# State-space stage of a decoder layer: the residual added by TensorE as transposes of x in the output unit's accumulation, and copied out by ScalarE

## What is computed

```python
hs = x @ W_in_states.T;  gate = x @ W_in_gates.T           # 1024 channels
hs = silu(causal_conv(hs, 4 taps) + conv_b)
dt = softplus((hs @ W_dt.T) @ W_dtproj.T + b_dtproj);  B = hs @ W_b.T;  C = hs @ W_c.T
s[l] = exp(A * dt[l]) * s[l-1] + dt[l] * B[l] * hs[l]      # 16 states for each channel
y = sum over the states of s * C + hs * D
out = (y * silu(gate)) @ W_out.T
x1 = x + out                                               # then the layer norm
```

## Time and profile before

| | |
|---|---|
| median of 3 runs | 3223.22 us (3222.08 to 3226.16) |
| the profiled execution | 3223.97 us, span 3222.1 us |
| state-space stage | 0 to 1747 us of the span |
| busy share of the span | PE 93%, DVE 87%, ACT 75%, POOL 65% |

### The profile page before, as it was taken

The page is one execution under the profiler, slowest core; times in us unless marked ns, Lnnn a source line. Parts: engine busy times, 40 slices in busy tenths (PEclk is TensorE's granted clock), DMA queues, the critical chain, the costliest instruction groups (busy, mean ns, idle before and its releaser), DMA issues. The chain is left out here.

```text
span 3222.1 us, 47346 instructions
## 1 busy us (share of the span) xinstructions
PE 3000.6 (93%) x16101; PEld 1827.8 (57%) x16134; DVE 2795.2 (87%) x3637; ACT 2410.8 (75%) x4531; POOL 2094.2 (65%) x1207
## 2 busy tenths in 40 slices
PE   7899999999999999999985899999999999699998
PEld 5777677777777677777753344444444443244444
DVE  6999999999999999999996878777887877288886
ACT  4888888888888888888872377677677667577786
POOL 5999999999999999999995243343344333100000
PEclk9999999999999999999996899999999999899999
DMA  4102220222012210222024455555556553221111
GB/s 173 45 32 79 80 73 18 79 83 79 26 65 79 80 62 29 79 80 83 15 96 137 148 171 168 186 158 177 177 154 179 168 178 92 82 93 47 46 42 36
DMA packets 164385, 311.93 MB, mean 97 GB/s; under 512 B 22736, under 2 KB 80208, under 8 KB 164000
## 3 DMA queue, kind: packets, MB, share of 16 engines
q1 hardware_dynamic: 158784, 299.53, 29.0%
q10 hardware_dynamic: 5360, 9.38, 1.0%
HBM read 217.16 MB, written 91.69 MB: 96 GB/s over the span
## 5 line engine op out<-in xcount | busy, mean ns | idle before, releaser
L830 POOL TENSOR_TENSOR bu<-du,bc 128x1024 f32<-128x1024 f32 x512 | 1198.9, 2370 | 30.4 <-DMA bc<-bc_scratch 28.5
L708 ACT ACTIVATE states<-dt,negA 128x256 f32<-128x256 f32 x2048 | 853.1, 463 | 238.7 <-DVE hc L926 227.9
L914 DVE TENSOR_TENSOR_SCAN states<-states,bu 128x512 f32<-128x512 f32 x704 | 821.5, 1213 | 10.6 <-ACT states L708 8.7
L1565 DVE TENSOR_REDUCE mmax<-s_ps 128x2 f32<-128x1024 f32 x512 | 624.8, 1224 | 205.6 <-PE s_ps L1284 186.7
L1409 ACT ACTIVATE pt<-s_ps 128x512 f32<-128x512 f32 x1024 | 573.5, 598 | 293.6 <-PE s_ps L1293 280.4
L926 DVE TENSOR_TENSOR hc<-states,bc 128x512 f32<-128x512 f32 x704 | 446.4, 676 | 0.4 <-DMA bc<-bc_scratch 0.4
L526 PEld LDWEIGHTS y_ps<-id_sb,hc 128*128 128x128 f32 x2816 | 331.5, 143 | 121.7 <-DVE hc L926 56.1
L526 PE MATMUL y_ps<-id_sb,hc 128*128 128x128 f32 x2816 | 377.5, 277 | 22.1 <-DVE hc L926 22.1
L1293 PE MATMUL s_ps<-qst,kst 105*128 105x512 bf16 x1024 | 379.1, 384 | 15.5 <-ACT pt L1409 5.1
L839 POOL TENSOR_TENSOR hp<-hp,bc 128x1024 f32<-128x1024 f32 x160 | 379.5, 2372 | 1.8 <-DVE hp L914 1.8
L914 DVE TENSOR_TENSOR_SCAN hp<-states,bu 128x512 f32<-128x512 f32 x320 | 372.5, 1206 | 5.2 <-ACT states L708 5.2
(11 more groups left out here) (172 smaller groups left out, 4237.4 us busy)
## 6 DMA issues: line engine op xcount, KB each, us to landing
bc<-bc_scratch SPq DMA_DIRECT2D x128, 512.0 KB, 5.1
stack_d<-parts SPq DMA_DIRECT2D x180, 256.0 KB, 3.0
qst<-stack_d SPq DMA_DIRECT2D x64, 384.0 KB
kst<-stack_d SPq DMA_DIRECT2D x64, 384.0 KB
x<-xres SPq DMA_DIRECT2D x31, 512.0 KB, 5.3
w_raw<-in_w_ffn SPq DMA_DIRECT2D x48, 256.0 KB, 2.7
w_raw<-in_w_ffn SPq DMA_DIRECT2D x16, 768.0 KB, 7.3
xT_sb<-in_xT SPq DMA_DIRECT2D x16, 512.0 KB, 6.0
```

The costliest lines, as they stand in the source:

```text
L708: a = act.activation(states[:, bank, first:first + SEQ], dt[:, t, :], ACT.Exp, scale=negA[:, t, c * NS + n:c * NS + n + 1])
L830: pool.tensor_tensor(bu[:, buf, :].rearrange("p (n l) -> p n l", n=NS), du[:, t % (2 * GRP):t % (2 * GRP) + 1, :].to_broadcast([P, NS, SEQ ...
L914: dve.tensor_tensor_scan(dst, src, bu[:, BU_OF[k][0], cols], 0.0, ALU.mult, ALU.add).then_inc(scan_done, 1)
L1565: dve.tensor_reduce(mmax[:, u // HG, c:c + 2], s1_ps[:, pair], AX.X, ALU.max).then_inc(s1_free, 1)
```

## The change

x is no longer loaded in rows of tokens for the sum, but once more from `xT`, where channels are rows: `xres` becomes [128, 2, 4, 128], and its load is two DMAs of 256 KB with runs of 512 bytes in place of one of 512 KB with runs of 2 KB. At the end of each `o` unit PE adds four transposes of 128x128 of `xres` to the same accumulation (with the identity as the other operand), after a wait for the load. ACT copies the bank to `xres` in `evacuate`, at the place that the table gives (after the decays of step 27 and of step 0). The last batch's `o` is still copied by DVE, now without an addition. The array `x` is no longer an input.

```diff
@@ load_xres (SP)
-                sp.dma_start(xres[:, :, :], at(x, b).rearrange("(i p h) -> p i h", p=P, h=HID)).then_inc(xres_in, 16)
+                src = at(xT, b).rearrange("(p k i l) -> i p k l", p=P, k=HK, i=SEQT)
+                for i in range(SEQT):
+                    sp.dma_start(xres[:, i], src[i]).then_inc(xres_in, 16)
@@ unit (PE)
                     elif kind == "o":
-                        m = pe.matmul(proj[:, :], y[:, par, k, i * P:(i + 1) * P], wout_sb[:, k, :], start=start, stop=stop)
+                        pe.matmul(proj[:, :], y[:, par, k, i * P:(i + 1) * P], wout_sb[:, k, :], start=start, stop=False,
+                                  skip_group_check=True)
+                if kind == "o" and hi == n:
+                    pe.wait_ge(xres_in, (f + 1) * SEQT * 16)
+                    for k in range(HK):
+                        m = pe.matmul(proj[:, k * P:(k + 1) * P], xres[:, i, k, :], id_sb[:, :], start=False, stop=(k == HK - 1),
+                                      is_transpose=True, skip_group_check=True)
@@ evacuate and its caller (ACT)
+                elif kind == "o":
+                    act.activation(xres[:, i].rearrange("p k l -> p (k l)"), proj[:, :], ACT.Copy).then_inc(ev["o"], 1)
-                        if kind != "o":
-                            evacuate(bank, kind, i, batch, side)
+                        evacuate(bank, kind, i, batch, side)
@@ body and tail (DVE)
-            def add_residual(bank, b, i):
-                dve.wait_ge(mm["o"], seq("o", b, i))
-                if i == 0:
-                    dve.wait_ge(xres_in, (b + 1) * 16)
-                dve.tensor_tensor(xres[:, i, :], xres[:, i, :], proj_banks[:, bank, :], ALU.add).then_inc(ev["o"], 1)
+            def last_out(i):
+                dve.wait_ge(mm["o"], seq("o", BATCH - 1, i))
+                dve.tensor_copy(xres[:, i].rearrange("p k l -> p (k l)"), proj_banks[:, 1 + i, :]).then_inc(ev["o"], 1)
-                    for bank, kind, i, batch, _ in due(b, par, k):
-                        if kind == "o":
-                            add_residual(bank, batch, i)
```

More of the change, by code:

```diff
@@ L140, with state_space_phase @@
     assert GRP * CPT * (_j - 1) - 1 <= _at < GRP * CPT * _j, (_j, _at)
-def state_space_phase(nc, xT, x, w_in, w_bc, w_dt, w_dtproj, w_out, chan, ident, w_ffn, bc_scratch, w_scales, x1,
+def state_space_phase(nc, xT, w_in, w_bc, w_dt, w_dtproj, w_out, chan, ident, w_ffn, bc_scratch, w_scales, x1,
                       ctxt, mask, wq, wk, chan_qk, stack_d, mask_d, x1n_d):
@@ L174, in state_space_phase @@
         xT_sb = sb("xT_sb", [P, HK, SEQ])
-        xres = sb("xres", [P, SEQT, HID])
+        xres = sb("xres", [P, SEQT, HK, P])
         xpad = sb("xpad", [P, 2, TAPS - 1 + SEQ])
@@ L357, in load_xres @@
             def load_xres(b):
-                sp.dma_start(xres[:, :, :], at(x, b).rearrange("(i p h) -> p i h", p=P, h=HID)).then_inc(xres_in, 16)
+                src = at(xT, b).rearrange("(p k i l) -> i p k l", p=P, k=HK, i=SEQT)
+                for i in range(SEQT):
+                    sp.dma_start(xres[:, i], src[i]).then_inc(xres_in, 16)
             def store_x1(b):
-                sp.dma_start(at(x1, b).rearrange("(i p h) -> p i h", p=P, h=HID), xres[:, :, :]).then_inc(x1_out, 16)
+                sp.dma_start(at(x1, b).rearrange("(i p h) -> p i h", p=P, h=HID),
+                             xres.ap().rearrange("p i k l -> p i (k l)")).then_inc(x1_out, 16)
             def load_piece(b, i):
@@ L453, in _ @@
                 sp.wait_ge(ev["o"], seq("o", BATCH - 1, i))
-                sp.dma_start(last[:, i], xres[:, i]).then_inc(x1_out, 16)
+                sp.dma_start(last[:, i], xres[:, i].rearrange("p k l -> p (k l)")).then_inc(x1_out, 16)
             sp.wait_ge(x1_out, BATCH * 16 + 16)
@@ L983, in tail @@
                 for i in range(SEQT):
-                    add_residual(1 + i, BATCH - 1, i)
+                    last_out(i)
             over_batches(dve, front, body, tail)
@@ L1994, in build @@
     x1n_d = dram("x1n_d", (BATCH * SEQ * HID,))
-    state_space_phase(nc, ins["xT"], ins["x"], ins["w_in"], ins["w_bc"], ins["w_dt"], ins["w_dtproj"], ins["w_out"],
+    state_space_phase(nc, ins["xT"], ins["w_in"], ins["w_bc"], ins["w_dt"], ins["w_dtproj"], ins["w_out"],
                       ins["chan"], ins["ident"], ins["w_ffn"], dram("bc_scratch", (2 * STATES, SEQ)), w_scales, x1,
@@ L2021 @@
     arrays = {
-        "x": x,
         "xT": x.reshape(BATCH, SEQ, HK, P).transpose(0, 3, 2, 1).reshape(BATCH, SEQ, HID),
```

## The result

| | before | changed |
|---|---|---|
| median, 5 runs each on one chip | 3223.71 us | 3253.93 us (3248.76 to 3257.79) |
| ratio, 95% interval | | 1.0093 (1.0079 to 1.0107) |
| the profiled execution | 3223.97 us | 3257.79 us, span 3256.0 us |

The changed kernel is slower by 30 us; the forecast was 21. The profiled execution of the changed kernel is the slowest of its five. Of its 33.9 us more of span, 31.2 lie in the state-space stage: the fill that follows the stage's tail on DVE starts at 1748.09 us before and at 1779.27 after. The other 2.7 us lie behind the stage, and a second profile of the same kernel, shown further down, doesn't have them, so nothing ties them to the change.

The account below looks back on a forecast made before the run. It took POOL's 104.22 us a batch as the bound, with PE's cycle growing to 104.7. The longer cycle, boundary and tail add 6 us and clock falls 15: 21 on the profiled 3223.97, median 3244, range 3223 to 3256.

Parts of the forecast that it names:

- What bounds the kernel: State-space stage: POOL's own work, 104.22 us a batch, sets the period, so less DVE work can't shorten it.
- The cycle of 104.02: Second cycle before the change, in us: DVE from step 4 to o1's addition, PE's d1, ACT to `xpad`, PE's c0 to step 4's sum.
- rival D: Faster: with DVE resting more, 42 large POOL operations shorten by 20 ns each, gaining 8 us, to 3215; chance 0.05.
- The transposes, 0.87 us a batch: On PE, eight pipelined transposes a batch add 0.87 us, 0.43 for each output unit, none hidden.
- The wait that goes and the one that comes: Batch boundary: d1 stops waiting for DVE; c0 waits for `xpad` behind o1's copy, a 9.5 us path, starting 0.9 us later.
- The period without the clock: State-space stage: PE's new cycle takes 104.7 us a batch, 0.5 over POOL's 104.22, before any clock falls.
- rival B: The cycle is longer but the clock holds: 6 us slower, 3229 (3226 to 3232); chance 0.21.
- The clock: PE idles 2.7 us ahead of c0; nine falls to 1.2 GHz in thirteen batches, 1.7 us each, cost 15 us.
- The rule against the forecast: The skill warns only of longer PE idle gaps; by it the clock holds, but rows at 2.03 and 2.18 us speak against it.
- The boundary and the tail: Last batch: DVE two additions ahead, -1.2 us; POOL's wait shorter, -0.6; tail's transposes, +0.9.
- DMA, nothing: Load of x: one more DMA and shorter runs cost nothing; were it three times slower, 6 us once.
- Rival E: Worse: ACT's wait for o0 delays step 28's scan, or transposes behind a 512-column matmul aren't pipelined; over 3256, chance 0.06.

Follow-up runs that it names:

- LAG 2: Against the changed kernel, ACT copies the output units one step later, o1 behind the decays of step 1: 3224.01 us, ratio 1.0000 to the kernel before.
- the kernel with the stretch filled: The changed kernel plus five matmuls of 256 columns, read by nothing, ahead of c0's wait in each batch from 2 on: 3230.44 us.
- The kernels with 2.21 and 2.73 us in the old code: The kernel before with an extra ACT table load ahead of s0's copy, the second also with a spare copy, lengthening c0's wait: 3243.57 and 3258.39 us.
- the edits: On the changed kernel, cumulatively: LAG 2, one POOL product moved to DVE, then d1 placed at step 2: 3224.01, 3218.02 (step 14 moved), 3199.72 us.

## Why the prediction was right, and where it was off

*What bounds the kernel.* Right for POOL: less work on DVE didn't shorten anything (the run with DVE's copy, and LAG 2, both at 104.2). The cycle of 104.02 is only in part as described: 1.19 us more on its DVE part made it 104.62 and not 105.2, and with POOL relieved it ran at 104.25. Two small things in the working are off and don't enter the sum: POOL's idle ahead of `du` is 0.16 us in the earlier trace rows, not two or three tenths, and rival D's own numbers give 104.15 - 103.4 = 0.75 us a batch, not 0.6.

*The transposes, 0.87 us a batch.* Right: four of them stand in 1015.94 - 1015.50 = 0.44 us, and without them the period is 0.87 shorter. The instructions of two lines in the changed kernel (shortest, median and longest ns, first and last start), the first for this and the second for the tail:

```profile
L510 PE MATMUL proj<-id_sb,xres x128: 272/273/273, 252.1 to 1774.9; 128*128 128x128 f32 x128
...
L957 DVE COPY xres<-proj x2: 691/692/692, 1773.1 to 1775.2; 128x512 f32<-128x512 f32 x2
```

Each takes 273 ns and one starts every 109. The Trainium skill, "TensorE: Matmul & The Clock Gate", Part 4, gives about 275 ns for a transpose in one kernel. The trace agrees with it as the duration of one (273 ns). The page doesn't say that the next one starts only then; that was the prediction's reading, and the 1.3 us a batch more that would have come of it aren't there.

*The wait that goes and the one that comes.* Right within 0.1 us: 9.5 us forecast from the sum behind o1 to c0, 9.53 measured; idle 2.7, measured 2.77; ACT at the copy about 2, measured 1.97; no wait ahead of d1.

*The period without the clock.* 104.7 forecast, 104.6 in the kernel with the stretch filled. That kernel as a whole is 7.1 us slower than before, where rival B had +6. Rival B had the right size and the wrong clock.

*The clock.* This is the term that was mis-sized: 15 us forecast, about 25 measured in the profiled execution. c0 of batch 2 is 0.97 us late (277.99 before, 278.96 after; forecast 0.7) and that of batch 14 is 30.2 late (1527.83, 1558.02). The twelve periods between them are 5.5 us longer than before in the kernel with the stretch filled, that is without falls. The remaining 23.7 us are twelve falls: seven of 1.7, two of 1.4 to 1.5 and three of 3.0. The thirteenth, of 1.7, comes behind c0 of batch 14. The price of a fall, read in the second batch of the kernel before, held in eight of thirteen and nearly in two. Two things failed: the count, nine where all thirteen fell, and the single price, since in three of thirteen the clock came back later. The count can't be had from a trace of before. The kernels with 2.21 and 2.73 us in the old code had 3 and 1 in thirteen in their profiled executions, the one without transposes 10, the changed one 13 twice.

*The range.* That 3253.93 lies in it is partly luck. All thirteen falls at 1.7 us, on top of rival B's 3229, make 3251; the 5 us above that, up to 3256, had no term in the working, and the measured median lies in them.

*The rule against the forecast.* The Trainium skill, "TensorE: Matmul & The Clock Gate", "Why this matters for your kernels", warns only of longer gaps; by it rival B would have come true. The runs decide against it: stretches of 2.77, 2.73 and 2.21 us ended in falls, the first in most batches and the other two in some.

*The boundary and the tail.* -0.9 us forecast in sum. From c0 of batch 14 to the end of the stage the changed kernel loses 1.0 us, and 1.7 of that is the thirteenth fall: -0.7. POOL's wait in the last batch is 2.13 us, 2.62 before; DVE's copy in the tail (L957 above) takes 692 ns, about what the addition took in the earlier trace rows (0.68 us), so nothing came of its lost operand. Part by part these weren't separated by runs.

*DMA, nothing.* PE has no wait for the load of x in the changed trace; LAG 2, with the same loads, is at 1.0000.

*Rival D, POOL's operations shorten.* `bu` has a median of 2363 ns, 2368 before: 5 ns, not 20, and POOL isn't the late one any more.

*Rival E* named ACT's wait for o0 and transposes behind a large matmul. The second doesn't show. The first does, but costs nothing: ACT waits 2.53 us for o0, and once a batch DVE then waits for ACT's decays, not at the scan of step 28 but at that of step 31. DVE's timeline:

```profile
1011.88 2.35 DVE L924 TENSOR_TENSOR_SCAN states<-states,bu 128x512 f32<-128x512 f32 x2 [0.49 <-ACT states L719]
```

The kernel with LAG 2 has the same wait of 0.49 us and is at 1.0000. The profiled execution came out at 3257.79, above the range, by the longer falls and the 2.7 us behind the stage.

## What to carry to other kernels

Moving a copy to an engine with spare time can cost far more than the copy: what counts is what stands behind it in that engine's order and when its input is complete. Follow the path from the input's end to the next instruction that another engine waits for, and put the copy one step later if the consumer of the bank allows it. Where two or three cycles are within two per cent of each other, write all of them down with their periods before spending an edit on one; here the edits gave 0, then 5 to 6, then 18 us, the most only when the last of them was cut. And look at what a change does to TensorE's idle time in one piece, not only to its sum: two waits of 1.75 and 0.82 us were harmless, one of 2.77 cost three times what the path itself did.

## What the runs showed of the hardware

Single idle stretches of 2.2 to 2.8 us, between stretches of nearly full work, can drop TensorE's granted clock to 1.2 GHz: 3 of 13 at 2.21 us, 1 of 13 at 2.73 in one kernel, 10 of 13 at 2.77 (one of the three that held was 2.59) and 13 of 13 at 2.77 in two others. At the 1.75 us that stood once a batch in the kernel before it held in all thirteen. A fall that came at c0's start (at most 0.1 us ahead of it) or behind it cost 1.6 to 1.7 us. One that came while PE was still idle cost 1.4 to 1.6 when it was 0.25 to 0.56 us ahead of c0 (six falls in the two profiles of the changed kernel), and 3.0 when it was 0.63 to 0.77 us ahead (six more; behind these the clock stayed low for longer). Executions of one kernel with such stretches differ by up to 19 us (3244.84 to 3264.15), where the kernel before, run beside it, stays within 7 (3219.12 to 3226.33 over 21 runs); what decides whether a given stretch drops the clock stays open.
